# One core, two gated attention blocks and two mixtures: attention loops written out, first contexts loaded in the setup, second mixture's first layer by channel

## The chip, the cores and the metric

The kernel runs on one core of a Trainium2 chip. Its engines are PE (TensorE: matrix multiplications and transposes, with weight loads as PEld), DVE (VectorE), ACT (ScalarE), POOL (GpSimd) and SP (SyncE, which here only issues transfers). Each engine works through its own list of instructions, and engines wait for each other on semaphores. The metric is the device time of one execution in microseconds, the median of several. The matrix engine runs at one of two clocks, 1.2 or 2.4 GHz; the profile prints the granted share of the upper one (0.5 or 1.0, or a mean in between).

## What is computed

x is 16 sequences of 256 rows of 128 values (4096 rows). There are 16 contexts of 1601 rows of 96 values. Four blocks are added to x one after another, each behind a gate tanh(g):

1. A cross attention with 4 heads. Every row keeps its 32 largest of 1601 scores per head, takes their softmax, averages the heads, and drives a FiLM-modulated state-space layer (a long convolution) and a feed-forward layer.
2. A mixture of 8 experts with limited capacity, one 128x128 matrix each.
3. A cross attention with 16 heads of width 8 over the same contexts.
4. A mixture of 8 experts, top 1, each with a hidden layer of 512:

```python
gate_scores = x @ Wg + bg
onehot = one_hot(argmax(gate_scores))
h = relu(einsum('btd,edh->beth', x, W1) + b1)
y = einsum('beth,ehd->betd', h, W2) + b2
out = einsum('betd,bte->btd', y, onehot)
```

## The kernel before

The program is a chain of phases. Between two phases all engines meet at a barrier, so a phase starts when the slowest engine has ended the one before it.

**Setup.** `setup_phase` loads weights, builds tables for the convolution, and for each of the 16 contexts turns it (PE transposes, ACT copies to `ctxT`) and computes keys and values of the second attention, which go to DRAM. SP's `load(b)` (L181) fetches context b into one of two buffers `s_ctxn`; in the loop at L202 it fetches b+2 for b below 14. SP saves keys (L207) and values (L209) of each context. The last work is on POOL: eight small transfers `kern<-turns` (L267), a read back (L270), a write to `kernpad` (L273), each waited for. Then come the barrier and the clearing of semaphores.

**First attention.** `attention0_phase` handles a batch (sequence and its context) in eight slots, one for each head and half of the 256 rows. In a slot PE makes 128x1601 scores (L852), ACT copies them out of PSUM (`scores_out_of`, L964), DVE finds the 32nd largest (L1076 on pieces, L1110 to L1114 on the candidates), POOL makes the cut from it (L717 to L719), ACT, POOL and ACT again blank what is below and take the exponential (L971, L735, L977), and DVE adds heads up in pairs (`add_pair`, L1136). A check on ties runs beside it: ACT counts (L985), PE sums (L860), ACT copies the count (L991), DVE reads it into a register (L1068) and branches over a rare general path (L1069, `dve.If`). Between the slots PE turns sums, multiplies by the context, and turns the next batch's context (L800), which ACT copies (L927). `walk` (L662) gives all five engines the same order: batch 0 written out, then a hardware loop over seven pairs of batches (`eng.Fori`, L666), so that batches 1 to 14 run in the loop, then batch 15 written out. In the loop batch numbers, and thresholds of the waits, are registers. SP's `load` (L673) fetches a context in two pieces and a row of the mask (L684); contexts 0 and 1 are fetched at the phase's start, after POOL has signalled `ready` (L704), on which PE waits too.

**Second attention.** PE, ACT and DVE are written out; POOL (values spread, keys split, L1972) and SP (transfers, L2033) run in hardware loops.

**Second mixture.** `mixture1_phase` normalises the 4096 rows (DVE L2384), turns them (PE L2456, ACT L2540), scores the gate (PE L2463), and DVE computes for each row its place in a list sorted by expert. POOL scatters the rows to DRAM (32 times L2354). Then 39 slots of 128 rows of one expert each follow. For slot s PE's order is: first layer (`first`: 512 columns with the rows as weights, L2493, and the bias by a matmul of three bf16 parts, L2495), second layer of slot s-1 (L2511, its bias L2513), four transposes of the hidden values (`turn_hidden`, L2503), transpose of the rows of slot s+2 (L2487). ACT applies relu (L2554) and copies the turned rows (L2546); DVE copies the turned hidden values out of PSUM (`turned`, L2430) and finishes the rows (`finish`, L2436); POOL scatters them to the output (L2361). The expert's number is read into a register of PE (L2517). Before that POOL splits both biases into three parts (L2346, L2348), which SP passes through DRAM. One semaphore `w_in` stands for gate weights and both expert weights (2 MB each); PE waits for it before its first transpose, DVE before the gate.

## Time and profile before

| | us |
|---|---|
| median of three runs (lowest, highest) | 3036.39 (3034.26, 3049.46) |
| the profiled execution | 3046.81 |
| its span from first to last instruction | 3045.3 |
| busy in the span: PE, DVE, ACT, POOL | 2531.6 (83%), 2224.1 (73%), 2081.6 (68%), 1250.3 (41%) |
| instructions in the span | 64460 |

The phases follow each other, so a share over the whole span says little; each stage has to be read by itself. The profile's rows name a group as line, engine, operation, tiles, shapes and count, then busy time and the mean of one in ns, then the idle time of the engine just before it and what ended it. "issue" is idle time for which the profile shows no releaser. In a timeline row the first number is the start in us from the span's start, the second the length. In the trace the setup tiles are called `s_...`, those of the second mixture `e_...`.

### The profile page before, as it was taken

What the parts mean: (1) busy time and instruction counts of PE and PEld (TensorE: products, weight loads), DVE (VectorE), ACT (ScalarE), POOL (GpSimd) and SP (SyncE); (2) the same over time, 40 slices, a digit from 0 to 9 for tenths busy, and PEclk for the clock granted to TensorE, in tenths of its full rate; (3) what the DMA queues carried; (4) which work ended last, traced back from release to release, by engine and by line L of the source; (5) the groups of instructions that cost most, each with busy time, mean ns of one, the idle gap of its engine ahead of it and who ended that gap; (6) DMA issues with size and microseconds to landing.
All of it is one profiled execution on the core that took longest, in us unless ns stands there. A gap on an engine that the chain in (4) does not pass through costs nothing. (4 is left out here: it accounts for less than half of the span.)

```text
span 3045.3 us, 64460 instructions
## 1 busy us (share of the span) xinstructions
PE 2531.6 (83%) x19758; PEld 1285.0 (42%) x19758; DVE 2224.1 (73%) x8194; ACT 2081.6 (68%) x3430; POOL 1250.3 (41%) x1598
## 2 busy tenths in 40 slices
PE   7958888888888888768787589999999999998278
PEld 5734556555555655535422123333333333333245
DVE  8728777778787777536544989999999999990322
ACT  5739888888888888614322078888888888888022
POOL 1427777777777777613100502322222232000432
PEclk9968888888888888788888589999999999999589
DMA  8820000000000000081440214333333333220321
GB/s 234 264 67 1 23 13 14 12 12 12 12 22 12 14 12 12 6 293 42 57 114 26 82 41 97 104 104 91 94 96 91 103 100 103 66 42 3 96 69 45
DMA packets 159409, 205.50 MB, mean 67 GB/s; under 512 B 74512, under 2 KB 127054, under 8 KB 159082
## 3 DMA queue, kind: packets, MB, share of 16 engines
q1 hardware_dynamic: 148732, 161.85, 19.8%
q0 software_dynamic: 10352, 39.92, 3.9%
q8 instruction: 132, 2.16, 0.3%
q14 instruction: 193, 1.57, 0.2%
HBM read 135.21 MB, written 66.62 MB: 66 GB/s over the span
## 5 line engine op out<-in xcount | busy, mean ns | idle before, releaser
L2143 ACT ACTIVATE pb<-sps 128x512 f32<-128x512 f32 (+1 forms) x1664 | 892.0, 597 | 232.4 <-PE sps L2085 224.3
L2166 DVE TENSOR_REDUCE mx<-wps 128x2 f32<-128x802 f32 x1024 | 949.5, 988 | 49.7 <-PE wps L2058 34.7
L1076 DVE MAX8 cand<-sc 128x8 f32<-128x46 f32 (+1 forms) x4480 | 603.0, 199 | 175.2 <-issue 101.4
L852 PE MATMUL scores<-ctxT,qT 97*128 97x512 f32 (+1 forms) x1024 | 472.2, 614 | 93.0 <-ACT sc L964 79.7
L2100 PE MATMUL ops<-pb,va 128*9 128x256 f32 x6656 | 516.0, 382 | 10.9 <-ACT ot L2149 7.1
L852 PEld LDWEIGHTS scores<-ctxT,qT 97*128 97x128 f32 x1024 | 219.7, 224 | 360.6 <-issue 262.7
L1942 POOL COPY va<-XX 128x128 f32<-128x128 f32 (+1 forms) x208 | 49.9, 293 | 648.4 <-PE ops L2100 640.5
L735 POOL TENSOR_TENSOR prf<-sc,prf 128x1601 f32<-128x1601 f32 x64 | 229.7, 3589 | 137.5 <-ACT prf L971 137.5
L735 POOL TENSOR_TENSOR prs<-sc,prs 128x1601 f32<-128x1601 f32 x64 | 230.6, 3603 | 10.2 <-ACT prs L971 5.1
L2058 PE MATMUL wps<-FO,Y 56*128 56x401 bf16 x1024 | 187.9, 357 | 50.4 <-DVE mx L2166 35.5
L827 PE MATMUL misc<-diag,prs 128*128 128x128 f32 (+1 forms) x1664 | 224.2, 288 | 5.9 <-issue 4.3
L827 PEld LDWEIGHTS misc<-diag,prs 128*128 128x128 f32 (+1 forms) x1664 | 205.1, 197 | 21.6 <-issue 18.2
L985 ACT ACTIVATE side<-sc,below 128x1601 bf16<-128x1601 f32 x128 | 207.8, 1624 | 1.6 <-POOL below L729 1.4
L964 ACT COPY sc<-scores 128x1601 f32<-128x1601 f32 x128 | 189.1, 1477 | 27.0 <-PE scores L852 26.1
L2058 PE MATMUL wps<-XX,Y 56*128 56x401 bf16 x1024 | 181.3, 343 | 27.2 <-DVE mx L2166 18.9
L2100 PEld LDWEIGHTS ops<-pb,va 128*9 128x9 f32 x6656 | 99.2, 88 | 203.2 <-issue 99.8
L2085 PE MATMUL sps<-Y,FO 59*128 59x256 bf16 (+1 forms) x1664 | 170.9, 277 | 5.3 <-DMA Y<-guards 5.1
L2085 PE MATMUL sps<-Y,XX 59*128 59x256 bf16 (+1 forms) x1664 | 172.9, 275 | 0.3
L729 POOL TENSOR_SCALAR below<-slack,top 128x1 f32<-128x1 f32 x128 | 129.0, 1008 | 13.0
L2085 PEld LDWEIGHTS sps<-Y,XX 59*128 59x128 bf16 (+1 forms) x1664 | 56.6, 95 | 169.2 <-ACT pb L2143 156.2
L2085 PEld LDWEIGHTS sps<-Y,FO 59*128 59x128 bf16 (+1 forms) x1664 | 54.0, 95 | 174.2 <-ACT pb L2143 158.8
L2430 DVE COPY e_hrT<-e_ht 128x512 f32<-128x512 f32 x39 | 27.0, 692 | 134.0 <-issue 80.8
(411 smaller groups left out, 4064.1 us busy)
## 6 DMA issues: line engine op xcount, KB each, us to landing
FO<-keys SPq DMA_DIRECT2D x392, 50.0 KB
XX<-keys SPq DMA_DIRECT2D x392, 50.0 KB
keys<-kpb POOLq DMA_DIRECT2D x42, 400.2 KB, 3.6
toep<-kernpad SPq DMA_DIRECT2D x8, 2048.0 KB, 15.2
values<-s_vs SPq DMA_DIRECT2D x16, 832.0 KB, 6.0
XX<-values SPq DMA_DIRECT2D x16, 832.0 KB, 4.5
keysf<-s_kf SPq DMA_DIRECT2D x16, 800.5 KB, 3.8
Y<-queries SPq DMA_DIRECT2D x784, 8.0 KB
```

The lines of the kernel that those rows point to most:

```text
L729: g.tensor_scalar(below32[:, s % 2:s % 2 + 1], e, 2.0 ** -22, t32, ALU.mult, ALU.subtract).then_inc(below32_ready, 1)
L735: g.tensor_tensor(pr[s][:, :], sc[s % 4][:, :], pr[s][:, :], ALU.subtract).then_inc(kept_ready, 1)
L827: ins = t.matmul(m[0:kn(kt), (kt % 4) * P:(kt % 4) * P + P], pr[s][:, kt * P:kt * P + kn(kt)], diag[s // 2][:, :], start=(p == 0), stop=(p ...
L852: ins = t.matmul(scores[:, c:c + n], q, ctxT[par][0:C + 1, c:c + n], start=True, stop=True)
L964: s_.copy(sc[s % 4][:, :], scores[:, 0:NK]).then_inc(scores_out, 1)
L985: s_.activation(side[s % 2][:, :], sc[s % 4][:, :], ACT.Sign, bias=below32[:, s % 2:s % 2 + 1], accum_out=sides[:, s % 2:s % 2 + 1]).then_ ...
L1076: st.add(v.max(cand[s % 2][:, 8 + n:8 + n + 7 * NP + 1:NP], sc[s % 4][:, c:c + w]))
L2058: ins = t.matmul(buf[:, 512 * odd:512 * odd + WIN], qs[par][r, h + odd, q * P:q * P + P], ks[par][r, h // 2, (WIN - 1) * c:(WIN - 1) * c + ...
L2085: ins = t.matmul(sps[(UNITS * g + u) % SB][0:kn(kt), i, :], ks[par][r, h // 2, kt * P:kt * P + kn(kt)], qs[par][r, h, :], start=True, stop ...
L2100: ins = t.matmul(ops[VW * i:VW * i + DH1 + 1, 0:S], va[par][0:kn(kt), kt, 4 * g + i, :], pb[(UNITS * g + 2 * kt + i % 2) % 8][0:kn(kt), i ...
L2143: nc.scalar.activation(pb[(UNITS * g + u) % 8][0:rows_, :, :], sps[(UNITS * g + u) % SB][0:rows_, :, :], ACT.Exp).then_inc(p_ready, 1)
L2166: v.tensor_reduce(mx4[:, q, h:h + 2, c], both, AX.X, ALU.max).then_inc(work_read, 1)
```

## The change

- `walk` in the first attention gives all 16 batches written out; waits compare with constants. The POOL loop and the SP loop of the second attention are written out too. The work of each batch stays.
- The two context buffers (`ctxn`, `ctxT`) are allocated once for both phases. In the setup SP also fetches contexts 0 and 1 again while it handles batches 14 and 15, `load((b + 2) % B)`, and waits for them at its end. In the first attention SP fetches for batches 0 and 1 only the row of the mask, without waiting for `ready`.
- In the second mixture the first layer is computed with the weights as the stationary side: four products give the hidden values of 128 channels each, already turned. DVE copies the expert's 128x512 weights and its four bias columns out of the table ahead (`slab`), with the expert's number in a register of its own; ACT adds the bias in four relus that write `hrT` directly. The four transposes, DVE's copy, the bias product, and the three-part split of b1 go.
- Gate weights have a semaphore `g_in`; `w_in` is waited for after the gate. The bias b1 is fetched by channel (`b1T`, 4096 single elements).

```diff
@@ setup
             for b in range(B):
-                if b + 2 < B:
-                    sp.wait_ge(kv_ready, kv_number["c", b, 3] + 1)
-                    load(b + 2)
+                sp.wait_ge(kv_ready, kv_number["c", b, 3] + 1)
+
+                load((b + 2) % B)
...
             for i in range(2):
+                sp.wait_ge(ctx_in[i], 32 * (B // 2 + 1))
@@ first attention
         def walk(eng, step):
-            step(0, 0, 1, True, False)
-            with eng.Fori(0, (B - 2) // 2) as i:
-                step(2 * i + 1, 1, i + 2, False, False)
-                step(2 * i + 2, 0, i + 2, False, False)
-            step(B - 1, 1, None, False, True)
+            for b in range(B):
+                step(b, b % 2, (b + 1) // 2 + 1, b == 0, b == B - 1)
...
+            def load_mask(b, par):
+                sp.dma_start(ctxT[par][C:C + 1, :], k.maskrow[bass.ds(b, 1), :]).then_inc(ctx_in[par], 16)
...
             def step(b, par, visit, first, last):
-                if not last:
-                    load(b + 1, 1 - par, None if first else number(b, "u1'") + 1)
-
-            sp.wait_ge(ready, 1)
-            load(0, 0, None)
+                if not (first or last):
+                    load(b + 1, 1 - par, number(b, "u1'") + 1)
+
+            for b in range(2):
+                load_mask(b, b)
             walk(sp, step)
...
-                    pe.wait_ge(ctx_in[par], 48 * visit)
+                    pe.wait_ge(ctx_in[par], 48 * visit - 32)
@@ second attention
-            with pool.Fori(1, B // 2 - 1) as i:
+            for i in range(1, B // 2 - 1):
...
-            with sp.Fori(0, (B - 4) // 2) as i:
+            for i in range((B - 4) // 2):
@@ second mixture, SP and POOL
+            for dst, src in ((wg[:, :], a["L1_ffn_Wg"]), (bg[:, :], a["L1_ffn_bg"].partition_broadcast(P))):
+                sp.dma_start(dst, src).then_inc(g_in, 16)
+            for dst, src in ((w1[:, :, :], a["L1_ffn_W1"].rearrange("e d h -> d e h")),
                              (w2[:, :, :, :].rearrange("p e c d -> p (e c) d"),
-                              a["L1_ffn_W2"].rearrange("e (c p) d -> p (e c) d", p=P))):
+                              a["L1_ffn_W2"].rearrange("e (c p) d -> p (e c) d", p=P)),
+                             (b1T[:, :, :], a["L1_ffn_b1"].rearrange("e (c p) -> p e c", p=P))):
                 sp.dma_start(dst, src).then_inc(w_in, 16)
...
-            for whole, parts in ((b1, b1h), (b2, b2h)):
-                for n in range(3):
-                    st.link(g_.tensor_copy(parts[n][:, :], whole[:, :]))
-                    if n < 2:
-                        st.link(g_.tensor_tensor(whole[:, :], whole[:, :], parts[n][:, :], ALU.subtract))
+            for n in range(3):
+                st.link(g_.tensor_copy(b2h[n][:, :], b2[:, :]))
+                if n < 2:
+                    st.link(g_.tensor_tensor(b2[:, :], b2[:, :], b2h[n][:, :], ALU.subtract))
@@ second mixture, DVE
-            dve.wait_ge(w_in, 16 * 4)
+            dve.wait_ge(g_in, 16 * 2)
...
-            def turned(s):
-                dve.wait_ge(ht_ready, s + 1)
+            def slab(s):
+
                 if s >= 2:
-                    dve.wait_ge(y_ready, s - 1)
-                v.tensor_copy(hrT[s % 2][:, :, :], ht[s % 2][:, :, :]).then_inc(hrT_ready, 1)
+                    dve.wait_ge(hrT_ready, s - 1)
+                e = dve.value_load(whoi[0:1, s:s + 1], min_val=0, max_val=E - 1)
+                v.tensor_copy(b1s[s % 2][:, :], b1T[:, bass.ds(e, 1), :].rearrange("p o c -> p (o c)")).then_inc(slab_ready, 1)
+                v.tensor_copy(w1s[s % 2][:, :], w1[:, bass.ds(e, 1), :].rearrange("p o h -> p (o h)")).then_inc(slab_ready, 1)
...
             for s in range(SLOTS):
-                dve.wait_ge(x_in[s % XB], nth(s, XB))
-                turned(s)
-                if s:
-                    finish(s - 1)
-            finish(SLOTS - 1)
+                if s + 2 < SLOTS:
+                    slab(s + 2)
+                finish(s)
@@ second mixture, PE
-            pe.wait_ge(w_in, 16 * 4)
...
             begin(0)
+            pe.wait_ge(g_in, 16 * 2)
...
-            def first(s, e):
+            def first(s):
                 pe.wait_ge(xT_ready, s + 1)
+                pe.wait_ge(slab_ready, 2 * s + 2)
...
-                t.matmul(hp[s % 2][:, :], xT[s % 2][:, :], w1[:, bass.ds(e, 1), :].rearrange("p o h -> p (o h)"),
-                         start=True, stop=False)
-                t.matmul(hp[s % 2][:, :], one3[:, :], b1p[:, bass.ds(e, 1), :].rearrange("p o h -> p (o h)"),
-                         start=False, stop=True).then_inc(h_ready, 1)
+                for c in range(4):
+                    ins = t.matmul(hp[s % 2][:, c * P:c * P + P], w1s[s % 2][:, c * P:c * P + P], xT[s % 2][:, :],
+                                   start=True, stop=True)
+                ins.then_inc(h_ready, 1)
...
-                turn_hidden(s)
@@ second mixture, ACT
-                s_.activation(hr[s % 2][:, :], hp[s % 2][:, :], ACT.Relu).then_inc(hr_ready, 1)
+                for c in range(4):
+                    ins = s_.activation(hrT[s % 2][:, c, :], hp[s % 2][:, c * P:c * P + P], ACT.Relu,
+                                        bias=b1s[s % 2][:, c:c + 1])
+                ins.then_inc(hrT_ready, 1)
```

## Rows read from the trace of the kernel before

**Rows 1.** Windows of four stages: us, busy PE PEld DVE ACT POOL, PE clock, DMA, GB/s
```profile
200.50:260.90 60.40, 46.75 (x122) 22.84 (x123) 46.00 (x355) 43.08 (x49) 32.16 (x40) 0.62 0.00 1
260.90:1190.90 930.00, 784.96 (x3892) 517.06 (x3891) 736.64 (x5314) 807.51 (x1052) 699.17 (x880) 0.87 0.05 14
2813.90:2907.30 93.40, 20.77 (x99) 19.85 (x100) 30.05 (x126) 4.69 (x8) 48.36 (x61) 0.50 0.30 95
2907.30:3035.60 128.30, 126.10 (x663) 77.39 (x663) 36.83 (x78) 33.66 (x78) 36.73 (x38) 0.97 0.20 56
```

**Rows 2.** Windows of an even and an odd batch of the looped attention
```profile
858.10:922.00 63.90, 55.43 (x280) 36.94 (x280) 52.50 (x381) 57.53 (x75) 49.88 (x64) 0.89 0.05 14
922.00:991.20 69.20, 56.85 (x281) 36.81 (x281) 52.83 (x383) 57.87 (x75) 50.18 (x64) 0.85 0.05 14
```

**Rows 3.** Timeline (start, us, group, idle before), DVE: batch end without, with back edge
```profile
872.76 0.33 DVE L1076 MAX8 cand<-sc 128x8 f32<-128x46 f32 x2 [0.35 <-DVE cand L1076]
...
941.17 0.33 DVE L1076 MAX8 cand<-sc 128x8 f32<-128x46 f32 x2 [3.20 <-issue]
```

**Rows 4.** Timeline, ACT: scores copies after either batch boundary
```profile
875.17 1.48 ACT L964 COPY sc<-scores 128x1601 f32<-128x1601 f32 x1
...
883.06 1.48 ACT L964 COPY sc<-scores 128x1601 f32<-128x1601 f32 x1
...
940.72 1.48 ACT L964 COPY sc<-scores 128x1601 f32<-128x1601 f32 x1
...
945.72 1.63 ACT L971 ACTIVATE prf<-sc,cutoff 128x1601 f32<-128x1601 f32 x1 [2.33 <-POOLq L720]
...
950.48 1.47 ACT L964 COPY sc<-scores 128x1601 f32<-128x1601 f32 x1
```

**Rows 5.** Timeline, setup end and first attention start
```profile
169.16 0.59 POOL L270 DMA_DIRECT2D turns<-kern  x1 [5.58 <-DMA kern<-turns]
...
181.80 0.10 POOL L703 MEMSET plain<- 128x1 f32 x1
...
186.36 0.85 PE L800 MATMUL misc<-ident,ctxn 128*96 128x128 f32 x3 [24.44 <-DMA ctxT<-maskrow]
```

**Rows 6.** Timeline, second mixture, rows normalised and turned for the gate
```profile
2830.51 3.52 DVE L2384 TENSOR_SCALAR e_rows<-X,e_mv,e_rstd 128x128 f32<-128x128 f32 x4 [0.15 <-DVE e_rows L2384]
...
2834.14 1.12 PE L2456 MATMUL e_tp<-ident,e_rows 128*128 128x128 f32 x4 [0.56 <-DVEq L2387]
...
2839.92 1.12 DVE L2384 TENSOR_SCALAR e_rows<-X,e_mv,e_rstd 128x128 f32<-128x128 f32 x4 [0.15 <-DVE e_rows L2384]
```

**Rows 7.** Waits in the second attention: us in total, times, longest us
```profile
POOL va L1942 <- PE ops L2100: 518.8, 12, 63.3
```

**Rows 8.** Timeline, PE, one whole slot of the second mixture
```profile
2935.60 0.66 PE L2503 MATMUL e_ht<-ident,e_hr 128*128 128x128 f32 x4
2936.09 0.27 PE L2487 MATMUL e_tp<-ident,e_xs 128*128 128x128 f32 x1
2936.20 1.02 PE L2493 MATMUL e_hp<-e_w,e_xT 128*128 x2
2937.16 0.39 PE L2495 MATMUL e_hp<-e_b1p,e_one 3*128 x1
2937.47 1.16 PE L2511 MATMUL e_yp<-e_w,e_hrT 128*128 x8
...
2938.72 0.55 PE L2503 MATMUL e_ht<-ident,e_hr 128*128 128x128 f32 x3
```

**Rows 9.** Groups (busy us, mean ns), ACT timeline, one line (ns min/median/max): prices
```profile
L2361 POOL DMA_INDIRECT out_dram<-e_ob,e_xs x39 | 38.3, 983 | 95.9 <-DVE e_ob L2436 92.9 <-issue 3.0
...
L1593 DVE CAST q_p<-q_f 128x512 bf16<-128x512 f32 x24 | 10.2, 425 | 6.1 <-ACT q_f L1766 5.3 <-DVE n_q_var L1352 0.2
...
1438.15 1.64 ACT L1368 ACTIVATE hn<-xt,n_in_shift,n_in_rstd 128x128 f32<-128x128 f32 x4
...
L1068 DVEq TENSOR_LOAD <-doubts x128: 303/307/553, 224.6 to 1274.7; - x128
```

More of the change, by code:

```diff
@@ L130, in setup_phase @@
         wk1, wv1, bk1 = sb("wk1", [C, D]), sb("wv1", [C + 1, D]), sb("bk1", [P, 1])
-        ctxn = [sb(f"s_ctxn{i}", [P, KT, C]) for i in range(2)]
-        ctxT = [sb(f"s_ctxT{i}", [C + 1, NK]) for i in range(2)]
+        ctxn, ctxT = k.ctxn, k.ctxT
         kf = [sb(f"s_kf{i}", [P, NK]) for i in range(2)]
@@ L568, in sem @@
             return k.used[-1]
-        ctxn = [sb(f"ctxn{i}", [P, KT, C]) for i in range(2)]
-        ctxT = [sb(f"ctxT{i}", [C + 1, NK]) for i in range(2)]
+        ctxn, ctxT = k.ctxn, k.ctxT
         xn = [sb(f"xn{i}", [P, QT, D]) for i in range(2)]
@@ L2236, in mixture1_phase @@
         w2 = sb("e_w2", [P, E, 4, D])
-        b1, b2 = sb("e_b1", [E, HID]), sb("e_b2", [E, D])
-        b1h = [sb(f"e_b1h{n}", [E, HID], BF16) for n in range(3)]
+        b1T, b2 = sb("e_b1T", [P, E, 4]), sb("e_b2", [E, D])
+        w1s, b1s = [sb(f"e_w1s{i}", [P, HID]) for i in range(2)], [sb(f"e_b1s{i}", [P, 4]) for i in range(2)]
         b2h = [sb(f"e_b2h{n}", [E, D], BF16) for n in range(3)]
-        b1p, b2p = sb("e_b1p", [3, E, HID], BF16), sb("e_b2p", [3, E, D], BF16)
+        b2p = sb("e_b2p", [3, E, D], BF16)
         one3 = sb("e_one3", [3, P], BF16)
@@ L2264, in mixture1_phase @@
         xT = [sb(f"e_xT{i}", [P, P]) for i in range(2)]
-        hr = [sb(f"e_hr{i}", [P, HID]) for i in range(2)]
         hrT = [sb(f"e_hrT{i}", [P, 4, P]) for i in range(2)]
@@ L2269, in mixture1_phase @@
         hp = [ps(f"e_hp{i}") for i in range(2)]
-        ht = [ps(f"e_ht{i}", (P, 4, P)) for i in range(2)]
         yp = [ps(f"e_yp{i}") for i in range(2)]
         X, ident = k.X, k.ident
-        lgp, locp, cntp = hp[0], hp[1], ht[0]
-        w_in, bias_in, consts = sem("e_w_in"), sem("e_bias_in"), sem("e_consts")
+        lgp, locp, cntp = hp[0], hp[1], yp[0]
+        g_in, w_in, bias_in, consts = sem("e_g_in"), sem("e_w_in"), sem("e_bias_in"), sem("e_consts")
         halves_ready, halves_out, halves_in = sem("e_halves_ready"), sem("e_halves_out"), sem("e_halves_in")
@@ L2282, in mixture1_phase @@
         x_in = [sem(f"e_x_in{i}") for i in range(XB)]
[L2283 to L2285 removed]
+        xt_ready, xT_ready, h_ready, hrT_ready = sem("e_xt_ready"), sem("e_xT_ready"), sem("e_h_ready"), sem("e_hrT_ready")
+        slab_ready, y_ready, o_ready = sem("e_slab_ready"), sem("e_y_ready"), sem("e_o_ready")
         stored = [sem(f"e_stored{i}") for i in range(OB)]
@@ L2424, in _ @@
             dve.sem_inc(who_ready, 1)
-            def turned(s):
-                dve.wait_ge(ht_ready, s + 1)
+            def slab(s):
                 if s >= 2:
-                    dve.wait_ge(y_ready, s - 1)
-                v.tensor_copy(hrT[s % 2][:, :, :], ht[s % 2][:, :, :]).then_inc(hrT_ready, 1)
+                    dve.wait_ge(hrT_ready, s - 1)
+                e = dve.value_load(whoi[0:1, s:s + 1], min_val=0, max_val=E - 1)
+                v.tensor_copy(b1s[s % 2][:, :], b1T[:, bass.ds(e, 1), :].rearrange("p o c -> p (o c)")).then_inc(slab_ready, 1)
+                v.tensor_copy(w1s[s % 2][:, :], w1[:, bass.ds(e, 1), :].rearrange("p o h -> p (o h)")).then_inc(slab_ready, 1)
+            dve.wait_ge(w_in, 16 * 3)
+            slab(0)
+            slab(1)
             def finish(s):
+                dve.wait_ge(x_in[s % XB], nth(s, XB))
                 dve.wait_ge(y_ready, s + 1)
@@ L2475, in _ @@
             o = locp[:, 0:T * E]
-            t.matmul(cntp[:, 0, 0:E], all1[:, :], total[:, T - 1, :], start=True, stop=True).then_inc(loc_ready, 1)
+            t.matmul(cntp[:, 0:E], all1[:, :], total[:, T - 1, :], start=True, stop=True).then_inc(loc_ready, 1)
             t.matmul(o, before[:, :], ohb[:, :, :].rearrange("p j e -> p (j e)"), start=True, stop=False)
@@ L2479, in _ @@
                      ).then_inc(loc_ready, 1)
-            pe.wait_ge(halves_in, 32)
+            pe.wait_ge(w_in, 16 * 3)
+            pe.wait_ge(halves_in, 16)
             pe.wait_ge(who_ready, 1)
@@ L2523, in _ @@
                 e = expert(s)
-                first(s, e)
+                first(s)
                 if s:
                     second(s - 1, last)
-                turn_hidden(s)
                 if s + 2 < SLOTS:
@@ L2593, in flamingo_kernel @@
         k.sorted = dram("sorted", [SLOTS * P, ROW])
[L2594 removed]
+        k.b2p = dram("b2p", [3, E, D], BF16)
         with ExitStack() as layer0:
@@ L2626, in flamingo_kernel @@
                     k.tmask = sbf("tmask", [P, T])
+                    k.ctxn = [sbf(f"ctxn{i}", [P, KT, C]) for i in range(2)]
+                    k.ctxT = [sbf(f"ctxT{i}", [C + 1, NK]) for i in range(2)]
                     setup_phase(nc, a, k)
```

27 lines of the change are left out of this document (6 added, 21 removed).

## The prediction

> **What bounds the kernel now.** I read the windows of the stages first, because the phases follow each other behind barriers. What the change touches lies in four of them [rows 1]: batch 0 of the first attention, written out already (60.4 us), batches 1 to 14 in the loop (930.0 us, 66.4 a batch), the preparation of the second mixture (93.4), and its 39 slots (128.3). Next come the busy times in each. In the slots PE is busy 126.1 of 128.3 us and every other engine below 37: there PE is the bound and a matmul taken away is time. In the looped batches nobody is full (PE 785, ACT 808, DVE 737, POOL 699 of 930): that stage is a ring of waits between engines, and time comes off only where a wait on the ring goes. Then two neighbouring batches side by side [rows 2]: an even one takes 63.9 us and an odd one 69.2, with the same instructions within a few. What differs is the hardware loop, which turns round after each even batch.
>
> **The loop written out.** The timeline of DVE shows what a turn costs [rows 3]: at the end of an odd batch (no turn) DVE is idle 0.35 us, at the end of an even batch 3.20 us, with no releaser ("issue"). So 2.85 us a turn. Seven iterations turn six times, the last falls through. ACT shows how it reaches the ring: copies of scores that are 7.89 us apart after a plain boundary (875.17 to 883.06) are 9.76 apart after a turn (940.72 to 950.48), and between them ACT waits 2.33 us for POOL's cut, which waits for DVE's maximum [rows 4]. That is 1.87 us directly. The odd batch is longer by 69.2 - 63.9 = 5.3 us in all [rows 2]; the other 3.4 come later, where PE's clock falls (0.85 against 0.89 granted), and it isn't clear that they belong to the turn. So a turn is worth between 1.9 and 5.3 us; I take 3.5, the middle, and 6 x 3.5 = 21 us. Register arithmetic ahead of waits goes too; no row prices it. The nearest is the plain boundary, where clearing a semaphore, the register and the next wait are 0.35 us together [rows 3]; a quarter of that in all 112 slots would be 10 us. I take 2, as the work is mostly done while the engine is busy, with 0 and 10 as ends. Sum for batches 1 to 14: 23 us, bounds 0 below and above 35.4, which is 14 batches at the 63.9 us of the best one: 930.0 - 14 x 63.9. Nothing is added there but code: twelve more batches of it, for each engine. Batch 0 with its own branches over the rare path runs 60.4 us as written-out code [rows 1], faster than any looped batch (it has less to do), so I put the fetching of longer code at nothing; if that cover fails, see the rivals.
>
> **Contexts loaded in the setup.** PE's first transpose of the phase starts at 186.36 and waited for the mask's row, last of three transfers behind the contexts; POOL's last constant, after which `ready` is signalled, ended at 181.90 [rows 5]. With the contexts there, PE needs `ready` and a row of 6 KB, asked for at the phase's start, ahead of POOL's constants. It starts at about 182.0: 4.3 us less. The price is 1.2 MB more read near the end of the setup. SP issues them after saving batches 13 and 14 and has nothing urgent behind them; but the second load shares the queues with the saves and with POOL's small transfers, whose landing POOL already awaits for 5.58 us before 169.16 [rows 5]. If 0.6 MB beside the 1.6 MB that a batch saves lengthens this wait in proportion, it is 5.58 x 0.6 / 1.6 = 2.1 us; some falls into gaps of the queues, so I take 1 us, ends 0 and 2.1. Net: 3.3 us less, bounds 2.2 and 4.3.
>
> **Loops of POOL and SP in the second attention.** POOL waits 518.8 us there for PE, in 12 waits [rows 7]; SP is ahead of the buffers as well. A turn of 3 us is covered by that. I put this at 0, ends -3 and +3. If the cover were gone, 5 turns of about 3 us on each engine would be bought back, no more.
>
> **Gate awaited apart.** PE turned the first group after `w_in`, the second at 2834.14, when DVE had it ready; from there PE is the chain. DVE needed 3.52 us for this group while POOL split b1 beside it, and 1.12 us for a group without POOL [rows 6]. With only b2 (a quarter of the columns) split, I take 1.8. Starting with the second group 1.7 us sooner moves the whole stage by that; the first group doesn't matter as it only has to be earlier, which needs the wait moved. So 1.7 us, bounds 0 and 2.4. The 4096 single elements of b1T come after the weights and are needed 45 us later, at the first slab; the scatter on POOL hides them.
>
> **First layer by channel.** One slot of PE, by the starts of its groups [rows 8]: transposes of hidden values 0.49 (2935.60 to 2936.09), transpose of rows 0.11, first layer 0.96, its bias 0.31, second layer with its bias 1.25 (2937.47 to 2938.72); together 3.12. The new slot has no 0.49, no 0.31, and four products of 128x128 by 128 columns in place of 0.96. The second layer is exactly such four products: 1.25 less a bias of some 0.15, that is 1.10. The new slot is 1.10 + 1.25 + 0.11 = 2.46 us, if PE stays the bound; 2.3 if the four go as fast as the 512 columns did.
> Does it? ACT has four relus of 128 columns with a bias; four ACT operations of that size take 1.64 us in a row [rows 9], and the copy of the turned rows is one more, 0.41: 2.05, under 2.46. PE asks for hidden values 2.46 us after it made them; ACT has them after its 1.64 us and some latency, about 1.9. DVE drops its copy and takes on the slab: reading the number 0.31 us and some 0.4 of sequencer work behind it, the weights 0.43, by a 128x512 conversion from the same memory to the same [rows 9], the four bias columns less than that, 0.2, and the finish, within the 36.8 us / 39 = 0.94 that DVE now works per slot [rows 1]. At most 2.3 a slot. The slab for slot s+2 can start when relu(s) is done and must be there when PE comes to it, 1.25 + 0.11 + 1.10 + 1.25 + 0.11 = 3.8 us after the end of first(s) [rows 8]; I count 1.9 + 0.7 + 0.2 + 0.43 = 3.2. Slack 0.6 us.
> 38 slots save 38 x 0.66 = 25.1 us. At either end nothing overlaps the way through the transposes and DVE's copy: 0.49 us at full clock at the end, about twice that at the start, where the clock is still the lower one [rows 1], and a copy of some 0.55 both times, 2.6 in all. That makes 27.7 us for the stage, 128.3 to 100.6. Bounds: 3 (period as before, only the ends gain) and 33 (2.3 us a slot).
> A rule speaks against the slab. The scatter of a slot on POOL takes 983 ns [rows 9] and comes just as DVE copies weights. By the Trainium skill (SBUF - State Buffer, "SBUF: two separate sides") a DVE copy of fp32 between SBUF tensors may hold a port pair that POOL shares, and whoever comes second is fully blocked. The 3.52 against 1.12 us above agrees with it in kind.
>
> **The sum.** 23 + 3.3 + 0 + 1.7 + 27.7 = 55.7 us off the profiled execution's 3046.8, so 2991.1. The median of three runs, 3036.4, is 10.4 below that execution; I subtract the same there: 2980.7.
>
> **Rivals.**
> A, DVE and POOL block each other over the slab. DVE's weights copy then ends up to 0.98 us later [rows 9], 4.2 us after first(s) against the 3.8 that PE allows; the slot grows to about 2.75 us. For it: rows 6. Against: whether they meet depends on who comes first. 36 x 0.29 = 10.4 us less is gained: 2991.
> B, the turns were only a part of the ring: what DVE waits less at a boundary, it waits for ACT or for PE at its lower clock elsewhere. For it: ACT, PE and DVE all have idle time in a looped batch [rows 2]. Against: the 1.87 us on ACT itself [rows 4]. Then 7 us instead of 23: 2997.
> C, more than forecast: all batches run like the even one (35.4) and the slot takes 2.3 us (33 for the stage): 12.4 + 5.3 more: 2963.
> D, the first layer by channel doesn't do what it says, because DVE's chain of relu, number, bias and weights becomes the bound at 3.1 us a slot. Gain 3 instead of 27.7: 3005. It needs 0.65 us more than the slack.
> E, slower: the branches over the rare path. In the loop their targets are near; written out, 14 batches have 112 of them, each jumping over code. If such a jump leaves what has been fetched, it costs a turn's 2.85 us. The gain of 55.7 and the 15 us that a measurement needs are eaten from 71 / 2.85 = 25 stalls on. With one jump in three, 37, it is 105 - 56 = 49 us slower: 3085. Against: batch 0 takes 60.4 us with seven such jumps in written-out code [rows 1], where stalls of 2.85 us have no room.
> By the Trainium skill (Runtime: NRT & Kernel Launch, "Instruction fetch mechanics") instructions are prefetched in sequence, and a taken branch to a page outside the fetched two stalls. That names the turn's 3.20 us, and it is E's rule as well; which of the two it is for a short jump, batch 0 answers.
>
> **Chances.** Forecast 0.50, A 0.17, B 0.13, C 0.10, D 0.06, E 0.04. The forecast's own range, with a turn at 5.3 or 1.9 us and 2 us for the rest, is 2968 to 2992. The range takes in C, A, B and D and leaves out E and combinations: 2960 to 3008. A measurement of this kernel can tell about 0.5% (15 us) from no change; faster than 3021 are all but E and a case in which B and D both hold and more is lost: faster 0.93, same 0.03, slower 0.04.
>
> **What would show it.** Right: DVE's 3.20 us of "issue" before L1076 gone at every second boundary; the 14 batches 895 to 925 us; PE's first L800 at about 182 and POOL's read back at 169 to 172; a slot of 2.4 to 2.5 us with PE busy throughout. Wrong: idle DVE behind many branches (E); PE waiting for `slab_ready` (A, D), with POOL's scatter or DVE's copy longer than 983 and 430 ns under A; batches still alternating, or all at 66 us (B). The weakest number is the 3.5 us a turn.

## The result, and the profile of the changed kernel

The changed kernel takes 2964.4 us (median of four runs, 2952.7 to 2972.2), the kernel before 3035.3 beside it (median of four, 3030.0 to 3049.5): a ratio of 0.975, 95% interval 0.971 to 0.980. Measured again with five runs on another occasion it was 0.975 (0.972 to 0.978). The forecast of 2980.7 was 16 us too high. The profiled execution took 2972.2 us, 74.7 less than that of the kernel before.

The windows of the four stages, as in [rows 1] (us, busy PE, PEld, DVE, ACT, POOL with instructions, granted PE clock, share of the DMA engines, GB/s):

```profile
190.00:249.20 59.20, 45.37 (x123) 22.69 (x123) 45.78 (x354) 43.26 (x50) 32.20 (x40) 0.68 0.00 1
249.20:1153.30 904.10, 762.87 (x3891) 504.57 (x3891) 736.02 (x5316) 806.00 (x1051) 699.43 (x880) 0.90 0.05 15
2778.80:2870.50 91.70, 20.74 (x99) 19.86 (x100) 28.74 (x130) 4.68 (x8) 44.27 (x56) 0.50 0.32 96
2870.50:2960.40 89.90, 88.86 (x702) 80.87 (x702) 33.84 (x113) 54.73 (x195) 37.29 (x38) 0.97 0.29 80
```

Beside [rows 1]: batch 1 begins at 249.2 where it began at 260.9 (11.7 us), batches 1 to 14 take 904.1 in place of 930.0 (25.9), the preparation 91.7 in place of 93.4 (1.7), the slots 89.9 in place of 128.3 (38.4). What lies between batch 15 and the second mixture takes 1625.5 in place of 1623.1. That makes 11.7 + 25.9 - 2.4 + 1.7 + 38.4 = 75.3 us; the spans differ by 75.1. In batches 1 to 14 PE's busy time fell by 22 us with the same matmuls, while the granted clock rose from 0.87 to 0.90. In the slots PE is busy 88.9 of 89.9 us and still the bound.

One slot of the second mixture (start, us, engine, line, group, idle before):

```profile
2916.69 0.23 PE L2508 MATMUL e_yp<-e_b2p,e_one 3*128 x1
...
2916.85 0.33 PE L2488 MATMUL e_tp<-ident,e_xs 128*128 128x128 f32 x1
...
2917.01 0.35 DVE L2438 SCALAR_TENSOR_TENSOR e_ob<-e_yp,TG,e_xs 128x128 f32<-128x128 f32 x1 [0.85 <-PE e_yp L2508]
2917.01 1.06 PE L2497 MATMUL e_hp<-e_xT,e_w1s 128*128 128x128 f32 x8
...
2917.91 1.06 PE L2506 MATMUL e_yp<-e_w,e_hrT 128*128 x8
2917.93 0.43 DVE L2427 COPY e_w1s<-e_w 128x512 f32 x1
2918.11 1.14 ACT L2549 ACTIVATE e_hrT<-e_hp,e_b1s 128x128 f32<-128x128 f32 x4 [0.63 <-PE e_hp L2497]
2918.22 1.00 POOL L2356 DMA_INDIRECT out_dram<-e_ob,e_xs  x1 [1.20 <-DVE e_ob L2438]
...
2918.90 0.23 PE L2508 MATMUL e_yp<-e_b2p,e_one 3*128 x1
...
2919.05 0.33 PE L2488 MATMUL e_tp<-ident,e_xs 128*128 128x128 f32 x1
```

By starts on PE: first layer 2917.01 to 2917.91, 0.90 us; second with its bias 2917.91 to 2919.05, 1.14; turned rows 0.16. The slot is 2.20 us, where it was 3.12 [rows 8]. DVE's copy of the weights, begun at 2917.93, is done at 2918.36; the products that read it start at 2919.22. DVE has 0.85 us of waiting for PE left in the slot shown.

The start of the first attention, against [rows 5]:

```profile
167.58 0.59 POOL L270 DMA_DIRECT2D turns<-kern  x1 [6.22 <-DMA kern<-turns]
...
180.23 0.10 POOL L703 MEMSET plain<- 128x1 f32 x1
180.43 2.58 PEld L800 LDWEIGHTS misc<-ident,ctxn 128*96 128x96 f32 x13 [20.97 <-POOLq L704]
```

PE's first weights load 0.2 us after the start of POOL's last constant (before, its first matmul came 4.56 us after it). POOL's wait for its eight small transfers, ahead of the read back, grew from 5.58 to 6.22 us; the read back is still 1.6 us sooner than before, because the eight transfers went out 2.2 us sooner in this execution.

### The profile page after: what moved, and what is told of

It is laid out like the page before. It is cut to its first block and busy times, and to the rows that moved or that the text cites. A ratio compares the mean times of both kernels' runs of the same rounds, so it can differ in the third digit from the quotient of the medians.

```text
span 2970.2 us, 61087 instructions
## 1 busy us (share of the span) xinstructions
PE 2470.1 (83%) x19797; PEld 1278.1 (43%) x19797; DVE 2219.1 (75%) x8233; ACT 2100.9 (71%) x3547; POOL 1247.3 (42%) x1593
## 5 line engine op out<-in xcount | busy, mean ns | idle before, releaser
L852 PE MATMUL scores<-ctxT,qT 97*128 97x512 f32 (+1 forms) x1024 | 456.4, 596 | 94.4 <-ACT sc L964 82.3
L852 PEld LDWEIGHTS scores<-ctxT,qT 97*128 97x128 f32 x1024 | 213.6, 218 | 351.2 <-issue 239.3
L1136 DVE SCALAR_TENSOR_TENSOR prs<-prf,ratio,prs 128x1601 f32<-128x1601 f32 x64 | 119.8, 1871 | 0.1
```

The lines of the kernel that those rows point to most:

```text
L852: ins = t.matmul(scores[:, c:c + n], q, ctxT[par][0:C + 1, c:c + n], start=True, stop=True)
```

## The experiments

Every kernel is the changed kernel with one thing undone or altered; "expert 0" has two (the first layer back, and the second layer's addresses fixed), and so has the last. This table has their stages in us, read from the traces, one profiled execution each. A batch starts with its first copy of scores; "middle" is from batch 15's first copy to the second mixture's first instruction, "slots" from the first turned rows to the last finish:

| kernel | batch 1 starts | batches 1-14 | middle | preparation | slots | against before (95%) |
|---|---|---|---|---|---|---|
| before | 260.9 | 929.9 | 1623.1 | 93.4 | 128.2 | 1 |
| changed | 249.2 | 904.1 | 1625.5 | 91.7 | 89.9 | 0.975 (0.971 to 0.980) |
| changed, again | 252.9 | 902.8 | 1623.2 | 91.4 | 90.1 | 0.975 (0.972 to 0.978) |
| loop on all engines | 249.5 | 931.1 | 1621.3 | 91.6 | 90.1 | 0.983 (0.976 to 0.989) |
| loop on DVE alone | 251.1 | 927.8 | 1616.9 | 91.6 | 89.3 | 0.981 (0.979 to 0.984) |
| loop on the others | 250.7 | 920.7 | 1619.9 | 91.6 | 89.5 | 0.976 (0.972 to 0.980) |
| contexts late | 249.9 | 902.4 | 1619.5 | 91.5 | 90.1 | 0.975 (0.971 to 0.978) |
| first layer back | 248.9 | 903.5 | 1615.1 | 93.5 | 128.4 | 0.984 (0.980 to 0.989) |
| expert 0 | 246.2 | 903.4 | 1615.0 | 93.4 | 127.8 | one run |
| two copies | 242.3 | 902.6 | 1619.5 | 91.7 | 91.0 | one run |
| four copies | 243.8 | 903.6 | 1615.0 | 92.2 | 107.9 | one run |
| one wait for all | 243.2 | 903.8 | 1615.4 | 93.7 | 90.8 | 0.975 (0.971 to 0.978) |
| loops of the second attention | 242.2 | 907.2 | 1605.1 | 91.5 | 90.0 | 0.971 (0.968 to 0.975) |
| b2 on DVE | 242.5 | 903.4 | 1608.9 | 91.1 | 80.0 | 0.969 (0.966 to 0.972) |

The stages that the edits don't touch differ too: batch 1 starts anywhere from 242 to 253 us, batches 1 to 14 take 902.4 to 907.2 with the same code, the middle takes 1605 to 1626. So an edit is judged by its own stage, and the timed ratios only tell the larger ones.

**The loop of the first attention: all engines, DVE alone, the others alone.**

```diff
         def walk(eng, step):
-            for b in range(B):
-                step(b, b % 2, (b + 1) // 2 + 1, b == 0, b == B - 1)
+            step(0, 0, 1, True, False)
+            with eng.Fori(0, (B - 2) // 2) as i:
+                step(2 * i + 1, 1, i + 2, False, False)
+                step(2 * i + 2, 0, i + 2, False, False)
+            step(B - 1, 1, None, False, True)
```

> The changed kernel with one part undone: the first attention's batches 1 to 14 run in the hardware loop again, on all engines. The two profiles differ by 25.9 us in this stage (930.0 against 904.1). Theory T (six turns on DVE's part of the ring, 3.5 to 4.3 us each): the stage is back at 928 to 932 us, 24 to 28 us over the changed kernel, some 48 under the kernel before; DVE shows its 3 us of idle before the maxima six times again. Rival B (the turns are made up for elsewhere, the gain came with the earlier start or with the clock of that execution): the stage stays under 915.

> The changed kernel with the loop put back on DVE alone; SP, POOL, PE and ACT stay written out. In the trace of before DVE's sequencer needs 2.7 to 2.85 us at the loop's end, those of the others 0.06 to 0.26. Theory T1 (only DVE's turn costs): 22 to 26 us over the changed kernel, nearly as much as with the loop on every engine. Rival R (register arithmetic ahead of the waits on all engines is a good part): DVE alone brings 10 to 17.

> The counterpart: the loop on SP, POOL, PE and ACT, and only DVE written out. Theory T1: 0 to 3 us over the changed kernel, the stage at 904 to 907. Rival R: 9 to 16 us over it.

Measured: 931.1, 927.8 and 920.7 us for the stage against 904.1: 27.0, 23.7 and 16.6 us, each from one profile and so good to a few us. The first settles B: with the loop back, the stage is back where it was before. With the loop on DVE alone the batches alternate again, 64.8 and 68.2 or 68.3 us from batch 4 on, so a turn costs 3.5 us there (over the whole stage 23.7 / 6 = 3.9), and the idle time of [rows 3] is back in the same place:

```profile
930.05 0.32 DVE L1082 MAX8 cand<-sc 128x8 f32<-128x46 f32 x2 [3.18 <-issue]
```

So T1 was right for DVE (22 to 26) and R wrong (10 to 17). But the others alone cost 16.6, which T1 doesn't allow (0 to 3) and R nearly does (9 to 16). Neither theory fits both runs. DVE's own part shows in its waits (us in total, times, longest), here in the changed kernel and with the loop on DVE alone:

```profile
DVE cand L1076 <- issue: 71.4, 41, 4.3
```

```profile
DVE cand L1082 <- issue: 101.4, 46, 6.5
```

What the others lose isn't found so easily. PE seems to wait longer for nothing visible ahead of the weights for scores. First the changed kernel, then the loop on the others:

```profile
PEld scores L852 <- issue: 239.3, 798, 0.5
...
PEld scores L852 <- ACT ctxT L927: 13.8, 15, 0.9
```

```profile
PEld scores L858 <- issue: 256.7, 812, 1.0
```

The 17 us between 239.3 and 256.7 are mostly a change of name. The 14 waits more, one in each batch, stand ahead of the next batch's first scores; there the changed kernel waits just as long, 0.94 us against 0.98 in batch 1, and the profile puts it down to ACT's copy of the turned context. With both rows together it is 253.1 against 256.7, so this place explains 4 us at most. What else differs is spread out. With the loop on the others PE is busy 789 us, against 763 in the changed kernel and 765 with the loop on DVE alone, at a granted clock of 0.87 against 0.90 and 0.88:

```profile
251.10:1178.80 927.70, 764.90 (x3891) 502.30 (x3891) 737.66 (x5322) 808.40 (x1050) 700.90 (x882) 0.88 0.05 15
```

```profile
250.70:1171.40 920.70, 789.42 (x3892) 522.93 (x3891) 736.22 (x5317) 806.23 (x1051) 700.64 (x880) 0.87 0.05 14
```

Nor does it sit at the turns: batches 7 to 12, odd and even, take 66.3 to 66.7 us. Whether it is register work, on which of the four engines, and whether the lower clock is its cause or its consequence, no run here separates: the edit puts all four into the loop at once.

So there were two prices, DVE's turn (23.7) and something in every batch on the other engines (16.6), and together they cost 27.0 and not 40.3: they overlap. Undoing one after the other, the second brings only 3.3 after the first, or 10.4 the other way round. The timed medians are 2988.6, 2988.2 and 2972.6 us, that is 53, 54 and 69 under the kernel before beside them (3041.9), where the changed kernel lies 71 and 76 under its own. That is in line with the first two; for "the others" it can't decide, since 16.6 in the stage is less than what the other stages vary by.

**Contexts loaded at the attention's start.**

```diff
-                sp.wait_ge(kv_ready, kv_number["c", b, 3] + 1)
-                load((b + 2) % B)
+                if b + 2 < B:
+                    sp.wait_ge(kv_ready, kv_number["c", b, 3] + 1)
+                    load(b + 2)
@@ first attention, SP
-            for b in range(2):
-                load_mask(b, b)
+            sp.wait_ge(ready, 1)
+            load(0, 0, None)
```

> The changed kernel with one part undone: the contexts of batches 0 and 1 are loaded at the first attention's start again and not at the setup's end. The prediction's term: 3.3 us over the changed kernel (PE's first transposes at 184 to 186 in place of 180.4, setup's end 1 us sooner or the same). Rival S (the whole difference of the two profiles up to the first copied scores, 10.5 us, belongs to this edit: 5.9 in PE's start and 4.6 in a PE that runs at its lower clock for longer): the first copy of scores is back at 199 to 201 and the kernel 9 to 11 us longer. Of the setup's end, which came 1.6 us sooner in the changed kernel, the first says it stays at about 180.2 for POOL's last constant, the second that it goes back to 181.8.

```profile
169.69 0.59 POOL L269 DMA_DIRECT2D turns<-kern  x1 [5.57 <-DMA kern<-turns]
...
182.29 0.10 POOL L702 MEMSET plain<- 128x1 f32 x1
...
186.82 2.58 PEld L799 LDWEIGHTS misc<-ident,ctxn 128*96 128x96 f32 x13 [24.58 <-issue]
...
196.42 1.50 ACT L963 COPY sc<-scores 128x1601 f32<-128x1601 f32 x1 [3.10 <-PE scores L851]
```

PE's first weights load 4.53 us after the start of POOL's last constant, against 0.20 in the changed kernel; the edit's 4.3 us are real there. The first copy is at 196.4, 6.4 later than in the changed kernel, between the two theories, and batch 1 starts at 249.9, 0.7 later than in the first profile of the changed kernel and 3.0 sooner than in the second. The ratio is the changed kernel's. That looks as if the gain were lost, but the clock hides it. Batch 0 took 53.5 us here, with PE's clock granted at 0.78, against 59.2 at 0.68 in the changed kernel and 60.4 at 0.62 before [rows 1]. To see the edit one needs a kernel that loads the contexts early and was granted the same clock. "Expert 0" (further down) has the changed kernel's first attention and is one (both were granted 0.82 from PE's first transpose to the first copy of scores, and 0.78 in batch 0). Here are batch 0 without the edit, batch 0 of "expert 0", and the latter's start:

```profile
196.40:249.90 53.50, 39.70 (x122) 20.74 (x123) 46.43 (x360) 43.15 (x49) 32.13 (x40) 0.78 0.00 1
```

```profile
192.70:246.20 53.50, 39.71 (x123) 20.83 (x123) 46.60 (x361) 43.16 (x50) 32.22 (x40) 0.78 0.00 1
```

```profile
170.26 0.59 POOL L270 DMA_DIRECT2D turns<-kern  x1 [6.15 <-DMA kern<-turns]
...
182.86 0.10 POOL L703 MEMSET plain<- 128x1 f32 x1
...
183.06 2.58 PEld L800 LDWEIGHTS misc<-ident,ctxn 128*96 128x96 f32 x13 [20.87 <-POOLq L704]
```

From POOL's last constant to batch 1 it is 67.6 us without the edit and 63.3 with it: the 4.3 us pass through to batch 1 in full. The price shows too. POOL waits 5.57 and 5.58 us ahead of its read back in the two kernels that load the contexts late, and 6.15 to 6.42 in the twelve that load them early, so it is 0.6 to 0.8 us, and the edit is worth about 3.6 net. On top of that the same stretch takes anything from 62 to 72 us in the kernels with early contexts, by the clock that PE is granted in it. Of the 11.7 us by which batch 1 starts sooner than in the kernel before, 1.6 is POOL's last constant, 4.3 the edit, and the other 5.8 go with the clock (0.86 against 0.50 granted from PE's first transpose to the first copy of scores, 0.68 against 0.62 in batch 0). Whether the earlier start itself makes the higher clock more likely, one profile of each kernel doesn't tell.

**The first layer as before.** The mixture's old code, with the gate still awaited apart.

```diff
-                for c in range(4):
-                    ins = t.matmul(hp[s % 2][:, c * P:c * P + P], w1s[s % 2][:, c * P:c * P + P], xT[s % 2][:, :],
-                                   start=True, stop=True)
+                t.matmul(hp[s % 2][:, :], xT[s % 2][:, :], w1[:, bass.ds(e, 1), :].rearrange("p o h -> p (o h)"),
+                         start=True, stop=False)
+                t.matmul(hp[s % 2][:, :], one3[:, :], b1p[:, bass.ds(e, 1), :].rearrange("p o h -> p (o h)"),
+                         start=False, stop=True).then_inc(h_ready, 1)
```

> The changed kernel with the second mixture's first layer as before (rows of hidden values, four transposes, bias as three bf16 rows); the gate is still awaited apart. By the two profiles (slots 3.13 and 2.20 us, the stage 128.3 and 89.8 us): 36 to 40 us over the changed kernel. By the prediction's sizes 27.7. Between the ends: if the gain of before to after in this stage is partly the chip's state, under 35. The second group of the preparation on DVE: 3.5 us again beside POOL's split of b1 (theory: POOL's split delays it), 1.8 if the waits made the difference.

```profile
2784.11 3.52 DVE L2385 TENSOR_SCALAR e_rows<-X,e_mv,e_rstd 128x128 f32<-128x128 f32 x4 [0.15 <-DVE e_rows L2385]
```

```profile
2861.00:2989.40 128.40, 126.27 (x663) 77.41 (x663) 36.77 (x77) 33.66 (x78) 36.69 (x38) 0.97 0.20 56
```

The first is a row of DVE's timeline, the second the window of the slots. The slots are back at 128.4 us, 38.5 over the changed kernel; the whole gain of this stage is this edit. The preparation is back at 93.5, and DVE's second group at 3.52 us beside POOL's split, though the gate is awaited apart: the 1.7 us belong to the split of b1, not to the separate wait. In the changed kernel this group is:

```profile
2795.32 1.76 DVE L2379 TENSOR_SCALAR e_rows<-X,e_mv,e_rstd 128x128 f32<-128x128 f32 x4 [0.15 <-DVE e_rows L2379]
```

**The same, with the second layer always taking expert 0's weights and bias ("expert 0").** It asks why the unchanged second layer shrank from 1.25 to 1.14 us.

```diff
-                    t.matmul(yp[s % 2][:, 0:D], hrT[s % 2][:, c, :], w2[:, bass.ds(e, 1), c, :]...
+                    t.matmul(yp[s % 2][:, 0:D], hrT[s % 2][:, c, :], w2[:, 0, c, :],
```

> As the run before (first layer as in the kernel before), but the second layer always takes expert 0's weights and bias, so that its addresses are constants; part of the result is wrong by that. The unchanged second layer with its bias took 1.25 us a slot before and 1.14 after. Theory Q (register arithmetic for the addresses in PE's queue, which the slim first layer hides and the fat one doesn't): 1.14 here too and a slot of about 3.0 us. Rival: it comes from the order of matmuls on PE's array, then 1.25 and 3.13 stay.

```profile
2900.61 1.16 PE L2513 MATMUL e_yp<-e_w,e_hrT 128*128 128x128 f32 x8
...
2901.85 0.66 PE L2505 MATMUL e_ht<-ident,e_hr 128*128 128x128 f32 x4
```

Still 2901.85 - 2900.61 = 1.24 us, and a slot of 3.13. Theory Q falls: it isn't the register addresses of this layer. By the starts of the single passes in the traces, the 0.11 us lie behind the first of the eight: the second starts 0.21 us after it where the bf16 product of 512 columns runs ahead of the group, and 0.11 where an fp32 pass does. Why stays open.

**More copies in the slab.** The weights copied twice, and four times.

```diff
+                for _ in range(1):
+                    st.link(v.tensor_copy(w1x[:, :], w1[:, bass.ds(e, 1), :].rearrange("p o h -> p (o h)")))
                 v.tensor_copy(w1s[s % 2][:, :], ...).then_inc(slab_ready, 1)
```

> The changed kernel with the slab's weights copied twice on DVE (once to a tile that nobody reads): 0.43 + 0.07 us more of DVE in each slot ahead of the real copy. In the trace the real copy ends 0.86 us before PE's matmuls that read it. Theory (there is slack of about 0.6 us, the prediction's figure): the slot stays at 2.20 us. Rival D (DVE's chain is the bound or nearly so): 2.4 to 2.7. Rival A (a DVE copy and POOL's scatter exclude each other): POOL's scatter, 1.00 us, or the copies, 0.43 us, get longer, as the copies now lie over the scatter's span: 1.2 to 1.4 us for the scatter.

> The same with four copies: 1.5 us more of DVE in each slot, beyond any slack. DVE's own work per slot is then 0.35 + 0.44 + 0.17 + 4 x 0.43 + 3 x 0.07 = 2.9 us. Theory: the slot is DVE's work plus its latencies, 2.9 to 3.1 us, the stage 25 to 33 us longer, POOL's scatter still 1.0 and the copies still 0.43. Rival A: the slot over 3.3 us, with the scatter or the copies longer than in the changed kernel.

The slots take 91.0 and 107.9 us, 2.22 and 2.69 us each. Half a microsecond more on DVE cost 0.02: the slack was there (0.86 us in the rows above, 0.6 forecast), and D is out. With four copies DVE is the bound: over 60 us of slots it waits for no other engine before it finishes the rows (0.0 us, 22.3 in the changed kernel), and PE now waits, for 5.5 us, ahead of the first layer. I had put that slot at 2.9 to 3.1, counting 0.07 between copies that follow each other without it. Over the same 60 us the copies take 469 and 491 ns on the mean with four, 428 in the changed kernel, and the scatter 1079 for 997. The single ones say more. Here is a slot with two copies, scatter and copies together:

```profile
2910.73 0.98 POOL L2357 DMA_INDIRECT out_dram<-e_ob,e_xs  x1 [1.21 <-DVE e_ob L2441]
2910.80 0.43 DVE L2429 COPY e_w1x<-e_w 128x512 f32 x1 [0.31 <-issue]
2911.26 0.70 DVE L2430 COPY e_w1s<-e_w 128x512 f32 x1
```

The copy that begins 0.07 us into the scatter takes its usual 0.43 us. The one that begins 0.53 us into it takes 0.70 and ends 1.23 us after the scatter's start. With four copies 16 began 0.52 to 0.62 us into a scatter of 0.98 or 0.99 us and took between 0.61 and 0.72: each of them, too, ended 1.23 to 1.25 us after the scatter's start, as if it had been held until about 0.8 us (1.23 - 0.43, an estimate) and then ran at its usual speed. The scatter is longer where a copy runs over its start: 1.00 us where the copy ends 0.14 us into it, as in the changed kernel, and 1.20 to 1.24 where it ends 0.34 to 0.38 us into it. So each holds the other up, a copy by 0.29 us at most and a scatter by 0.25. By the Trainium skill (SBUF - State Buffer, "SBUF: two separate sides") the one that comes second is fully blocked. In kind the traces agree, but not for the whole instruction: a copy can begin and end inside a scatter undisturbed. Only parts of the scatter exclude it, one at its start and one that ends about 0.8 us after it. In the changed kernel the copy (2917.93 to 2918.36) meets only the first (scatter from 2918.22).

**One wait for all weights ahead of the gate.**

```diff
-            begin(0)
             pe.wait_ge(g_in, 16 * 2)
+            pe.wait_ge(w_in, 16 * 3)
+            begin(0)
```

> The changed kernel, but PE waits for all weights, b1 by channel among them, before its first transposes of the preparation, as the kernel before did for its weights; DVE still waits for the gate alone. In the changed kernel these transposes start at 2795.3 us and b1 by channel lands 16.6 us after its issue at 2781.5, so at 2798.1. Theory: 2.8 us later on PE; the preparation 1 to 3 us longer, 93 to 94.5 in place of 91.7. The prediction put the separate wait at nothing by itself and the 1.7 us on POOL's shorter split: with the first layer put back and the separate wait kept, the preparation was 93.5, as in the kernel before. If the separate wait had its own gain beside b1's late landing, more than 3 us.

```profile
2762.30:2856.00 93.70, 20.68 (x99) 19.95 (x100) 28.75 (x130) 4.68 (x8) 44.28 (x56) 0.50 0.31 94
```

2.3 us longer than the 91.4 of the run beside it: the separate wait brings nothing over the kernel before, but it pays for the late landing of b1 by channel, which the changed kernel put into the same semaphore.

**The loops of POOL and SP in the second attention.**

```diff
-            for i in range((B - 4) // 2):
+            with sp.Fori(0, (B - 4) // 2) as i:
@@ POOL
-            for i in range(1, B // 2 - 1):
+            with pool.Fori(1, B // 2 - 1) as i:
```

> The changed kernel with the loops of POOL and SP in the second attention put back. The prediction: 0, ends -3 and +3; the time from batch 15's first copy to the mixture's start was 1615 to 1626 us in nine profiles and stays there. Rival (their turns do hold up the transfers): 5 turns of 3 us, 15 more.

The second attention itself, from its first product of scores to its last, as windows; first with the loops back, then the changed kernel beside it:

```profile
1545.00:1565.00 20.00, 17.31 (x48) 5.64 (x47) 12.66 (x31) 4.62 (x10) 1.40 (x3) 1.00 0.06 20
1700.70:2747.00 1046.30, 994.72 (x12088) 332.64 (x12088) 923.45 (x1124) 899.25 (x1725) 202.96 (x290) 1.00 0.31 82
```

```profile
1560.00:1580.00 20.00, 17.31 (x41) 5.46 (x40) 10.27 (x26) 4.14 (x10) 1.40 (x3) 0.84 0.06 20
1725.20:2771.40 1046.20, 994.61 (x12087) 332.65 (x12088) 923.46 (x1124) 899.23 (x1725) 203.02 (x290) 1.00 0.35 82
```

1046.3 against 1046.2 us: the loops cost nothing. And yet this kernel is the faster by 15 us, 2952.4 against 2967.4, with ranges that don't overlap (2947.3 to 2958.4, and 2962.4 to 2972.2). The first row of each says where: in the stretch of the first mixture, ahead of the edit, PE is granted 1.00 here and 0.84 there, and gets through 48 matmuls in 20 us instead of 41. The phase that holds it, the same code in both, begins 11.6 us sooner in this kernel and ends 24.5 sooner. The edit doesn't reach it except by the code's place and the moment at which it begins; which of the two tips the clock stays open.

**A version with the last cheap things taken off.** PE waits for `ready` only before the first scores, and the second bias goes from PE to DVE.

```diff
-                t.matmul(yp[s % 2][:, 0:D], one3[:, :], b2p[:, bass.ds(e, 1), :].rearrange("p o d -> p (o d)"),
-                         start=False, stop=True).then_inc(y_ready, 1)
+                ins.then_inc(y_ready, 1)
@@ DVE, between slab(s + 2) and finish(s)
+                v.scalar_tensor_tensor(out=b2s[s % 3][:, :], in0=b2B[:, bass.ds(regs.pop(s), 1), :]...,
+                                       scalar=k.TG[:, 3:4], in1=xs[s % XB][:, D:2 * D], op0=ALU.mult, op1=ALU.add)
```

> The changed kernel with two more edits. The second layer's bias leaves PE: DVE adds gate times bias to the residual rows ahead of time, in the 0.85 us in which it waits for PE, from a copy of b2 broadcast over the partitions; POOL's split of b2 and its way through DRAM go. And PE waits for the constants (`ready`) only before the first scores, not before its first transposes. If PE stays the slots' bound, a slot loses its 0.16 us: 2.20 to 2.04 and 39 x 0.16 = 6.2 us less; the preparation 0.6 us less (second group of DVE 1.76 to 1.11); PE's first transposes 2.4 us sooner, of which 0 to 2.4 reach batch 1. In all 7 to 9 us less than the changed kernel. Rival: DVE (1.4 us a slot now, 0.35 and a number's arithmetic more) or ACT's ring becomes the bound, the slot stays at 2.15 to 2.25 and the gain is 1 to 3 us.

```profile
2845.90:2925.90 80.00, 79.01 (x663) 77.03 (x663) 44.25 (x151) 50.85 (x195) 42.00 (x38) 0.96 0.31 89
```

This is the window of the slots. The slot fell from 2.20 to 1.94 us (forecast 2.04), the stage from 90.1 to 80.0. By the starts of the single passes the bias product had come 0.21 us behind the last fp32 pass, where two fp32 passes are 0.11 apart, and took 0.16 to its own successor: so it cost about 0.1 us beside its own 0.16. The scatter takes 1.13 us on the mean here, with two DVE operations over it, and it doesn't matter. PE's first transposes came 1.0 us sooner beside POOL's constants, not 2.4. The kernel's time is 2944.1 us, ratio 0.969 (0.966 to 0.972), 23 under the changed kernel beside it; 10.1 in the slots and 0.4 in the preparation are the edit's, perhaps 1.0 at the start, the rest lies in batch 0 and in the middle, where the clock varies.

## Why the prediction was right, and where it wasn't

**The loop: 23 forecast, 25.9 to 28.3 measured** (27.0 in the one run that undoes it alone). The turn on DVE was right in place and in size: 3.5 us was called the weakest number, and the loop on DVE alone gives 3.5 us a turn by its late batches and 3.9 over the stage. The step that was mis-sized is register arithmetic: "a quarter of that in all 112 slots would be 10 us. I take 2". The loop on the other four engines costs 16.6 by itself, outside the bounds, but only 3.3 beside DVE's turn. I had priced it by DVE's boundary, and it arises without DVE in the loop. On which of the four it arises, and whether it is register arithmetic at all, stays open. That the 2 us came near in the sum is due to the overlap, not to the reasoning: luck. Batches no longer alternate: most take 64.8 us, which is 0.9 more than the best one before.

**Contexts: 3.3 forecast, about 3.6 found** where the clock was the same. PE's start came 4.3 us nearer to POOL's constants, as said (4.3). The price of 1 us at the setup's end is 0.6 to 0.8. The gain passes to batch 1 in full. The read back at 167.6 lies outside the 169 to 172 that I had named as a sign, since the setup ahead of it was sooner. What the prediction left out is the clock: from POOL's last constant to batch 1 the same code takes 62 to 72 us, so the term can't be read from one pair of profiles, nor from the timed ratios.

**POOL's and SP's loops: 0**, and 0.1 us measured in their stage.

**Gate and split: 1.7 forecast, 1.7 measured**, by the step named: DVE's second group 1.76 us, taken as 1.8. The separate wait is worth nothing but keeps 2.3 us of loss away.

**First layer: 27.7 forecast, 38.4 measured**, above even the upper bound of 33. The mechanism was right (PE stays the bound, transposes and bias go, DVE has slack, 0.86 us for 0.6), the new slot wasn't: 2.20 and not 2.46. The mis-sized term is "1.10", which I took from the second layer as it stood behind a bf16 product and in front of one. Eight fp32 passes of 128 columns start 0.11 us apart and need 0.90; the other 0.2 was a late first step and a late bias. So 0.20 less in the first layer, 0.11 less in the second, which now also stands behind fp32, and 0.05 more for the transpose of rows: 0.26. Over 38 slots that is 35.0 us, and 3.4 are left for the two ends, taken as 2.6. ACT's four relus take 1.14 us, not 1.64.

**The rivals.** A: DVE's copy and POOL's scatter do hold each other up, but by 0.3 us at most and not by the scatter's length, and in the changed kernel they nearly pass each other by: copies take 0.43 us, scatters 1.00 for 0.98. B: refuted, the stage follows the loop. C had the right size for the first layer's side (2.3 a slot, 2.20 measured) and too much for the loops (35.4); its 2963 is nearest to the time. D: refuted by two copies. E: refuted, 14 batches with all their branches took 904 us.

**What no term held** is the clock. The middle took 2.4 us more in the profile of the changed kernel than before, 17 less in another kernel with the same code there, and 20 less in the one whose loops in the second attention cost nothing. The measured 71 to 76 us therefore aren't the sum of the edits to better than some 12 us. By their own stages the edits are worth 27 + 38.4 + 1.7 + 0 + 3.6, about 71. That this meets the timed 71 (76 on the second occasion) so closely is chance.

## What to carry to other kernels

A hardware loop can cost at its turn, on the engine whose next work is awaited (3.5 us on DVE here, nothing on POOL and SP in the second attention), and in every pass of its body (16.6 us in 14 batches with PE, ACT, POOL and SP in the loop). The two overlap, so their single prices don't add. When a wait in one profile has no releaser and in another has one, compare the place and its length before calling it new. Price a matmul group by the starts of its passes in the middle of the group; its first and its last step belong to its neighbours, above all where fp32 and bf16 alternate. And before a timed difference of half a per cent is put down to an edit, or its absence to none, compare the stages that the edit doesn't touch and the clock granted in them: the gain of the early contexts shows only between profiles with the same clock.

## What was unexpected of the hardware

- The same code takes 1605 to 1626 us in the middle and batch 1 starts between 242 and 253 us, with the granted PE clock differing (1.00 against 0.84 in one stretch), and this goes by kernel: five and four runs of two kernels didn't overlap.
- A bf16 product of three rows and 128 columns, set behind fp32 passes, cost 0.26 us of a 2.20 us slot; from its start to the next product's it is 0.16.
- A DVE copy of 128x512 fp32 (0.43 us) and a POOL scatter (0.98 us) exclude each other only in parts of the scatter: 18 copies begun 0.52 to 0.62 us into one all ended 1.23 to 1.25 us after its start, while one begun 0.07 us into it wasn't held up.
